# Four edits to a timetable: output weights taken in parts further apart, twelve instead of six P tiles sent in one batch, a context fetch moved, and one weight split moved in the opening

## The reference

```python
# L0: x attends to ctx, heads of 64
attn = softmax(einsum('bhqd,bhkd->bhqk', qh * scale, kh) + add_attn, masked by keys)
x = layernorm(einsum('bhqk,bhkd->bhqd', attn, vh) @ w_o + x) * ln_g + ln_b
# SA: x attends to x under a mask; CA: x attends to ctx, heads of 32
x = ln(x + mha(x, x, sa_w..., mask));  x = ln(x + mha(x, ctx, ca_w..., None))
# FF
x = ln(x + linear(relu(linear(x, ff_w1, ff_b1)), ff_w2, ff_b2))
```

## Time and profile before

| | |
|---|---|
| median of 3 runs | 3891.62 us (3890.29 to 3897.64) |
| the profiled execution | 3889.44 us |
| its span | 3887.6 us |
| granted TensorE clock, mean | 0.994 |
| PE, DVE, ACT, POOL busy | 3737.7, 2703.7, 2233.5, 1950.1 us |

### The profile page before, as it was taken

One profiled execution on the slowest core, in us unless ns is written; L12 is line 12 of the kernel. 1 busy time (PEld: TensorE's weight loads), 2 busy tenths in 40 slices (PEclk: granted clock), 3 DMA queues, 4 the chain that ended last, 5 costly groups with the idle time before them and its releaser, 6 DMA issues.

```text
span 3887.6 us, 63400 instructions
## 1 busy us (share of the span) xinstructions
PE 3737.7 (96%) x20588; PEld 2779.1 (71%) x20588; DVE 2703.7 (70%) x5753; ACT 2233.5 (57%) x4852; POOL 1950.1 (50%) x1981
## 2 busy tenths in 40 slices
PE   9999999999999998999999998999999989999999
PEld 6776676677777766776676766667666768888887
DVE  6666665567776767888888887888888863444334
ACT  6555555555555556878878777777777752111111
POOL 5544444434544545777777656667676642112101
PEclk9999999999999999999999999999999999999999
DMA  6666667454555566666666547666666683122210
GB/s 200 201 188 195 200 195 201 132 151 131 141 136 136 133 187 171 171 170 167 170 171 167 148 145 189 174 167 160 168 162 168 176 223 95 60 67 71 67 29 33
DMA packets 867943, 584.64 MB, mean 150 GB/s; under 512 B 641824, under 2 KB 690976, under 8 KB 866592
## 3 DMA queue, kind: packets, MB, share of 16 engines
q1 hardware_dynamic: 853648, 538.63, 51.7%
q10 hardware_dynamic: 13968, 41.95, 3.4%
HBM read 189.29 MB, written 237.50 MB: 110 GB/s over the span
## 4 chain that ended last, share of the span: by engine, by line
PE 40%; ACT 6%; POOL 6%; issue 5%; DVE 5%; DMA 1%; SPq 0%; DVEq 0%; POOLq 0%; ACTq 0%
PE psV L1599 6%; POOL QS L2436 5%; PE psT L1568 4%; PE psS L1547 4%; PE psS L1492 3%; PE psS L1494 3%; PE psS L1493 3%; PE psJ L1492 3%; ACT PR L1879 2%; PE psJ L1494 2%; PE psJ L1493 2%; PE psT L1492 2%; PE psT L1494 2%; PE psT L1493 2%; ACT plain L1898 1%
## 5 line engine op out<-in xcount | busy, mean ns | idle before, releaser
L2436 POOL TENSOR_SCALAR QS<-QK 32x1024 fp32r<-32x1024 f32 (+2 forms) x1152 | 1237.2, 1074 | 865.1 <-DVE QK L2098 435.3
L1879 ACT ACTIVATE PR<-PR,MN 128x512 f32<-128x512 f32 x1536 | 1100.9, 718 | 587.6 <-DVE MN L2080 484.0
L2080 DVE CUSTOM_DVE_ANT_0 PR<-psS,RAW 128x512 f32<-128x512 f32 x1024 | 694.0, 682 | 411.4 <-PE psS L1544 321.5
L1568 PE MATMUL psT<-ID,PR 128*128 128x128 f32 x3912 | 598.0, 276 | 63.5 <-ACT PR L1879 58.3
L1568 PEld LDWEIGHTS psT<-ID,PR 128*128 128x128 f32 x3912 | 472.3, 141 | 198.1 <-ACT PR L1879 103.8
L1599 PE MATMUL psV<-plain 128*32 128x512 f32 (+1 forms) x3072 | 508.9, 611 | 15.0 <-DMA plain<-split_rows 8.1
L1547 PE MATMUL psS<-QS 128*128 128x512 f32 x1024 | 453.4, 444 | 25.2 <-DVE PR L2084 11.1
L2084 DVE TENSOR_SCALAR_CACHE_REDUCE PR<-psS 128x512 f32<-128x512 f32 x512 | 345.3, 683 | 104.3 <-PE psS L1547 102.3
L1918 ACT ACTIVATE PR<-psS,COLS 128x512 f32<-128x512 f32 x128 | 88.3, 690 | 565.4 <-PE psS L1494 565.4
L2176 DVE COPY plain<-psT 128x512 f32<-128x512 f32 x530 | 361.6, 682 | 0.0
L1898 ACT ACTIVATE plain<-psT 128x512 f32<-128x512 f32 x448 | 263.0, 587 | 87.9 <-PE psT L1568 86.4
(11 more groups left out here) (162 smaller groups left out, 8429.0 us busy)
## 6 DMA issues: line engine op xcount, KB each, us to landing
split_rows<-plain SPq DMA_DIRECT2D x366, 256.0 KB, 2.7
split_rows<-RAW SPq DMA_DIRECT2D x192, 256.0 KB, 2.5
x<-Y SPq DMA_DIRECT2D x96, 256.0 KB, 2.4
RAW<-x SPq DMA_DIRECT2D x96, 256.0 KB, 3.5
Y<-x SPq DMA_DIRECT2D x96, 256.0 KB, 3.3
kept_c<-R SPq DMA_DIRECT2D x32, 512.0 KB, 4.1
kept<-ROWS SPq DMA_DIRECT2D x32, 512.0 KB, 3.5
R<-kept_c ACTq DMA_DIRECT2D x8, 2048.0 KB, 8.6
```

Source lines behind the costliest of these rows:

```text
L1568: mm = nc.tensor.transpose(dst[:, kt * P:(kt + 1) * P], prob(st, k)[:, kt * P:(kt + 1) * P], ID[:, :])
L1879: nc.scalar.activation(prob(st, k), prob(st, k), ACT.Exp, bias=MN[:, k % 8:k % 8 + 1], scale=-1.0, accum_out=row_sums(st, SM, g)[:, qt, j: ...
L2080: nc.vector.tensor_tensor_reduce(out=prob(st, k), in0=psS[:, n % 2], in1=FB[:, k % NT], scale=-st.scale, scalar=BIG, op0=ALU.add, op1=ALU. ...
L2436: nc.gpsimd.tensor_scalar(to, pair, 1.0, 1.0, ALU.mult, ALU.mult).then_inc(stacked, 1)
```

## The change

- TAKES: the four parts of SA's output weights, in the first batch of SA, and of CA's, in the first batch of CA, are taken at slots 30, 38, 46 and 54 instead of 26, 29, 32 and 35.
- sent(): in the last batch of SA the tiles below 32 are considered instead of those below 16, so that tiles 16, 18, 20, 22, 24 and 26 are sent too. Tiles 18 and 24 are split by ACT, the other four by DVE.
- ENTER: the first context fetch of CA, which stands in the last batch of SA, moves from slot -38 to -29 of CA, that is from slot 26 to slot 35 of that batch.
- SEAM: in the opening the second block of Q's weights is split at -27.8 (high) and -27.4 (low) instead of -28.6 and -28.1. That of K stays at -28, and the first K projection is evacuated at -28.4 and -28.15.

```diff
@@ TAKES
-    ("first", 2): [("SA", "O", (26, 29, 32, 35))],
+    ("first", 2): [("SA", "O", (30, 38, 46, 54))],
     ("last", 2): [("CA", "Q", 42.2), ("CA", "K", 44.7), ("CA", "V", (24, 27, 30, 33))],
-    ("first", 3): [("CA", "O", (26, 29, 32, 35))],
+    ("first", 3): [("CA", "O", (30, 38, 46, 54))],
@@ ENTER
-    "C_TAKE": -38,
+    "C_TAKE": -29,
@@ sent
-    return tuple(k for k in range(16 if st.name == "SA" and b == B - 1 else st.steps) if k % every in SENT[st.name])
+    return tuple(k for k in range(32 if st.name == "SA" and b == B - 1 else st.steps) if k % every in SENT[st.name])
@@ SEAM[('first', 0)]
+        ('W_HI', ('L0a', 'Q', 1), None, 0): -27.8, ('W_LO', ('L0a', 'Q', 1), None, 0): -27.4,
```

## The result

The changed kernel takes 3899.39 us (median of 21 runs, 3890.85 to 3905.76), the kernel before on the same chip 3890.72 us (21 runs). The ratio is 1.0019, 95% interval 1.0013 to 1.0024: 5 to 9 us slower. The ratio lies just inside the 0.2% that was set as the bound of "no change", and the interval reaches beyond it. The forecast was "no change", but with +0.7 us instead of +7.4, and the median lies 0.4 us above the range. The profiled execution took 3897.83 us. PE, DVE and POOL are busy for less time than before and ACT for 0.1 us more, while the span grew by 8.4 us; what the change costs is waiting.

What follows compares the result with a forecast made beforehand. PE was taken to bound whole batches, with waits for a FETCH and a lowered clock at slots 36 to 40. Terms -3.3 - 4.9 - 1.7 + 10.0 + 0.6 = +0.7 us gave 3892.3 us, range 3883 to 3899.

Steps and rivals of the forecast that it cites:

- takes, SA's batch 0: SA's first batch, slots 36 to 40: falls from 11.25 to 7.98 us, 3.3 us less.
- takes, CA's batch 0: CA's first batch, slots 36 to 40: falls from 13.07 to 8.19 us, 4.9 us less.
- six tiles, slots 16 to 36: SA's last batch: sending six more tiles saves 1.7 us, bounds nothing and 2.2 us.
- slots 36 to 40 of SA's batch 7: SA's last batch: product waits for tile 26's FETCH beside the context; 9.07 becomes 19.05 us, +10.0.
- opening: Opening: DVE's evacuation and PE start one operation later, +0.6 us, bounds -1.9 and +0.8.
- The takes further apart: SA's and CA's first batches: spreading the weight parts frees tile 26's FETCH, 3.3 and 4.9 us less.
- the floor for SA: SA, slots 36 to 40: the undisturbed 7.98 us, with DVE busy all of the time.
- the new stall: SA's last batch, slot 36: PE waits for tile 26's FETCH, slowed by BOUNCE backlog and context; +10.0 us.
- Rival 4: SA's last batch: fourth V part delays context and FETCH, lower clock lasts longer; term +14.1, total 3896.4 us, chance 0.15.
- my lower bound: SA's last batch, slots 36 to 40: +3.1 us if the FETCH gets through ahead of the context.
- rival 1: SA's last batch: FETCH gets ahead of the context; term +3.1, total 3885.4 us, chance 0.20.
- Rival 2: SA's last batch: FETCH and context take turns, FETCH about 1.5 us later; term +4.6, total 3886.9 us, chance 0.12.

Runs made afterwards that it cites:

- The last experiment: Changed kernel with next part's row loads behind FETCH 26, ten tiles sent, SA's first weight part at slot 26.5, opening as before: 3879.11 us, ratio 0.9956 to before.
- with the context later: Changed kernel with the context's fetch at slot 39 instead of 35, behind the FETCH of tile 26: ratio 1.0001 to before.
- the repeat of the changed kernel: The changed kernel measured once more with no edit: ratio 1.0010 to the kernel before.
- last batch only: Kernel before with only twelve tiles sent in SA's last batch and the context's fetch at slot 35: ratio 1.0021.
- takes only: Kernel before with only the output weights' takes moved to slots 30, 38, 46 and 54 in SA and CA: ratio 0.9986.

## Why the prediction was right in its class and wrong in its sum

**The sum, term by term.** Means over the profiles of the table, against the terms of the prediction.

| term | predicted | measured |
|---|---|---|
| takes, SA's batch 0 | -3.3 | +0.7 (119.4 in four, 118.8 to 120.0; 120.1 in seven, 118.1 to 121.6) |
| takes, CA's batch 0 | -4.9 | -6.2 (119.2 in four, 113.0 in ten) |
| six tiles, slots 16 to 36 | -1.7 | -1.6 |
| slots 36 to 40 of SA's batch 7 | +10.0 | +11.8 (9.05 in five, 20.8 in four) |
| opening | +0.6 | +1.2 |
| sum | +0.7 | +5.9 |

The changed kernel was measured at +7.4 and +3.9 us (1.0019 and 1.0010); 5.9 lies between them. That the class was right is in part luck: the takes in SA and the stall missed by 4.0 and 1.8 us to the same side, and only CA's 1.3 us more than forecast made up for some of it.

**The step that failed** is in "The takes further apart": "only one part is in flight ahead of that FETCH and none beside it", from which I took the floor for SA, 3.3 us less. Its reason was read in CA and carried over to SA. In CA's batch 0 before, the FETCH of tile 26 itself was slow (7.7 us); in SA's it took 3.3 us as one alone does, and late was its BOUNCE, which took 6.4. For CA the term came out, though "none beside it" did not: in ten profiles the part, issued 1.5 us behind the FETCH of tile 24, is still in flight for 1.1 to 3.4 us when the FETCH of tile 26 goes out, and that FETCH lands in 4.4 to 5.6 us. In SA the same slot number puts the part 0.35 us behind the FETCH of tile 24, in a burst with a row load and a BOUNCE ahead of them and the FETCH of tile 26 behind. In seven profiles the part took 6.4 to 9.8 us to land, the FETCH 7.3 to 10.2, and the product started 1.2 to 4.1 us after slot 36. The bound "nothing if row loads and not the takes delay the FETCH" was there, but not this reason. The order of the issues would have told it: a slot is a place in a sorted list, and what is issued beside a step has to be looked up in each stage. The last experiment shows the price, in one profile: with the part elsewhere the wait and the clock's fall are gone. That the two are issued close together is not enough by itself: at slot 38 of the same batch a part went out within 0.4 us of a FETCH in three profiles, and they took 4.0 to 4.8 and 4.8 to 5.4 us. What in the burst of slot 30 makes the difference stays open.

**Right.** The six tiles (35.4 forecast, 35.48 measured), and slots 36 to 40 of CA's batch 0 at their undisturbed length: 7.43 us. Nearly right are the parts at slots 38 to 54 at no price. The last one has a small price at slot 68 (slot 4 of CA's batch 1), a place that the prediction named: a FETCH beside it and the context took 11.6 to 14.7 us in nine profiles, where it takes 7.3 to 7.9 without the part, and in three of the ten with it PE waits 0.6 to 1.2 us there, in none of the four without. The mean of batch 1 is 105.7 against 105.3 us.

**Right in size, partly wrong in reason: the new stall.** I took 12.15 us for a stretch with the BOUNCE's backlog alone, and 6.9 for the context. The FETCH did land 1.0 us behind the context, against 1.3 forecast, and the product stood 10.3 us against some 10. What the term lacked is the clock: I added the longer wait to a stretch at 0.86, and the four profiles show 0.68 to 0.77. Over them the product starts 11.2 us after slot 36, against the 10.7 of the forecast (3.8 in CA's batch 7 and 6.9), and the rest of the stretch takes 9.6 us instead of 8.3. Rival 4 had such a term, and its condition held: the fourth V part landed 3.0 to 5.4 us after the release. But the context took 8.0 to 10.3 us all the same, and not 2.5 more than 9.9.

The reason for the stall was wrong in part: without the context the profile shows 18.12 us for the stretch, not 12.15. The 3.33 us of CA's batch 7, on which my lower bound stood, were one draw from a wide spread: over ten profiles the product there starts 3.3 to 7.6 us after slot 36, and the FETCH of tile 24, ahead of it, took between 6.4 and 12.2 us to land with the same instructions around it. So the 6.9 us of rival 1, the FETCH ahead of the context, are not what the order of these two alone is shown to give: with the context later the stretch is 2.7 us below the mean of the four. What pays is the row loads' place: then BOUNCE 26 lands before the context is asked for.

**Rival 2, turns between the queues.** The FETCH of 256 KB released together with 2 MB took 10.2 us where one alone takes 3.4, about as long as the 2 MB. So the price of this rival was wrong, and so was the prediction's reading that the rows speak against turns. The packets of the two queues, counted from 2259 to 2261 us, 4 to 6 us after the release (q10 is ACT's queue with the context, q1 is SP's with the FETCH; packets, MB, share of the transfer engines), show it:

```profile
DMA packets 88, 0.81 MB, mean 406 GB/s; under 512 B 39, under 2 KB 39, under 8 KB 39
q10 hardware_dynamic: 49, 0.80, 93.9%
q1 hardware_dynamic: 39, 0.01, 2.2%
```

The counts are nearly equal (49 and 39; 52 and 49 in the repeat of the changed kernel, 54 and 48 in "last batch only"), but the context's packets hold 16 KB and the FETCH's 256 bytes. The rule of the Trainium skill ("DMA: Bandwidth & Descriptors", section "Queues, rings and completion order"), turns packet by packet, agrees with these counts. My estimate of some 5 us took the turns to share the bytes equally, which the rule does not say: in this stretch the FETCH has 1% of the bytes, and most of its 1024 packets went in the last 3 of its 10 us, when the context was nearly through.

**The opening.** The term was an operation of 0.68 to 0.78 us. The operation at that place took 0.69 to 1.33 us in the six profiles without the edit, and the two together 1.76 to 2.48 in the eight with it: the term is about 1.1 us instead of 0.7. The prediction had no term for the clock here, which fell in six of the eight and in one of the six; how much of the 1.2 that is, the spread does not let me tell.

## What to carry to other kernels

Before a transfer is moved by a slot number, look up in each stage what it will be issued beside: the same 512 KB took 4.2 us to land at slot 26.5 and up to 9.8 at slot 30, in a burst with a transposing fetch that somebody waits for. When a tile's way goes out to memory and back, look at the loads queued ahead of its first half; here moving four loads with a distant reader behind it made the changed kernel 18 us faster (0.9964 against 1.0010 in its repeat), more than any edit of the change. Count in packets, not bytes, what a small transfer must share with a large one. And a bound read from a single profile is one draw: where a stretch waits on transfers, read it in several executions before it becomes the end of a range.

## What the runs showed of the hardware

- The same instructions with the same transfers around them land in very different times. In CA's batch 7 BOUNCE 26 and FETCH 24 took 5.8 to 6.5 and 6.4 to 7.0 us in seven profiles, 8.5 to 8.8 and 9.1 to 12.2 in the other three; nothing between. From the first score to SA's first score the program took between 1416.9 and 1424.1 us over fourteen profiles, about as much as the whole effect of the change.
- A wait does not always cost the clock, and its length alone did not tell here. In SA's batch 0 before, PE stood from 1517.17 us, and the granted clock went to 0.50, the lower level of 1.2 GHz, at 1517.50, 0.3 us into a wait of 1.54 (0.70 over the stretch). In the changed kernel a wait of 0.69 us at the same place went with 0.82. In CA's batch 7 of "takes only" PE kept 2.4 GHz through a wait of 3.28 us (clock 1.00, 10.68 us for the stretch), and in the repeat, where the product started 3.55 us after slot 36, too (10.47 us); in "last batch only", with 3.51 us, it did not (0.86 and 12.10). The difference between the last two is 1.6 us.
- Two queues shared the transfer engines by packets and not by bytes: over 2 us 49 packets of 16 KB went beside 39 of 256 bytes, 0.80 against 0.01 MB.
- The same DVE subtraction of 128x512 at one place of the opening took 0.69 to 1.33 us in six profiles.
